# Where the tiles of a fused transformer kernel begin in SBUF: small ones first, large ones at multiples of 1024 bytes

## The reference

```
x = x + tanh(g_xattn[0]) * L0_xattn(ctx, ctx, layernorm(x))   # 16 heads of 16, softmax over the HEADS
x = x + tanh(g_ffn[0])   * L0_ffn(layernorm(x))               # silu(x Wg') * (x Wu') Wd', hidden 768, int weights / 127
x = x + tanh(g_xattn[1]) * L1_xattn(layernorm(x), ctx)        # 16 query heads, one key/value head, softmax over the context
x = x + tanh(g_ffn[1])   * L1_ffn(layernorm(x))               # x (W + lora)' + b
```

## Time and profile before

| | |
|---|---|
| time, median of 3 runs | 2446.94 us (2446.25 to 2447.63) |
| span of the profiled execution, first to last instruction | 2442.8 us, so 4.1 us less than the median |
| the 58 rounds of the loop, at 36.31 us each | 2106 us of the span |
| PE busy | 97% |
| DVE, POOL, ACT busy | 90%, 73%, 70% |
| granted TensorE clock | 0.996 of full speed, that is 2.4 GHz |

### The profile page before, as it was taken

The page is one execution under the profiler, slowest core; times in us unless marked ns, Lnnn a source line. Parts: engine busy times, 40 slices in busy tenths (PEclk is TensorE's granted clock), DMA queues, the critical chain, the costliest instruction groups (busy, mean ns, idle before and its releaser), DMA issues.

```text
span 2442.8 us, 70142 instructions
## 1 busy us (share of the span) xinstructions
PE 2357.7 (97%) x27814; PEld 2081.6 (85%) x27814; DVE 2205.6 (90%) x3678; ACT 1719.5 (70%) x3402; POOL 1773.4 (73%) x2512
## 2 busy tenths in 40 slices
PE   6899999999999999999999999999999999999897
PEld 5788888888888888888888888888888888888786
DVE  6879999999999999999999999999999999999963
ACT  4567777777777777777777777777777777777664
POOL 3667777777777777787777777777777777777653
PEclk9999999999999999999999999999999999999999
DMA  3000010010011010011001000001001001101000
GB/s 106 25 19 29 28 35 24 28 35 24 28 35 30 22 35 30 26 31 30 28 28 30 28 28 31 28 28 35 24 28 35 24 28 35 30 22 35 17 19 15
DMA packets 74326, 73.26 MB, mean 30 GB/s; under 512 B 6555, under 2 KB 73393, under 8 KB 74290
## 3 DMA queue, kind: packets, MB, share of 16 engines
q1 hardware_dynamic: 74290, 72.75, 9.5%
HBM read 54.90 MB, written 16.78 MB: 29 GB/s over the span
## 4 chain that ended last, share of the span: by engine, by line
PE 64%; DVE 19%; ACT 7%; POOL 7%; issue 2%; DMA 0%; POOLq 0%; SPq 0%; DVEq 0%; ACTq 0%
PE work L2136 13%; PE work L2137 11%; PE work L2138 11%; DVE m L1517 6%; PE scores L2229 6%; PE scores L2239 5%; PE work L2272 5%; PE work L2175 4%; DVE scores L1523 4%; ACT e L857 3%; POOL zt L417 3%; PE scores L2218 3%; ACT xn_D L814 3%; PE work L2153 2%; PE work L2159 2%
## 5 line engine op out<-in xcount | busy, mean ns | idle before, releaser
L857 ACT ACTIVATE e<-scores 120x1024 f32<-120x1024 f32 x512 | 513.4, 1029 | 88.3 <-PE scores L2239 56.6
L2136 PE MATMUL work<-xt_hi_B,w_hi 128*128 128x256 f32 x1536 | 456.5, 297 | 3.8 <-DVE y_lo_A L1497 1.6
L2137 PE MATMUL work<-xt_lo_B,w_hi 128*128 128x256 f32 x1536 | 430.2, 280 | 0.0
L2138 PE MATMUL work<-xt_hi_B,w_lo 128*128 128x256 f32 x1536 | 430.0, 280 | 0.0
L417 POOL TENSOR_TENSOR zt<-e 120x512 f32<-120x512 f32 x256 | 328.7, 1285 | 118.1 <-ACT e L857 112.1
L411 POOL TENSOR_TENSOR h_lo<-h_f,h_hi 128x256 fp32r<-128x256 f32 x384 | 279.5, 735 | 147.3 <-ACT h_hi L807 147.1
L1517 DVE TENSOR_REDUCE m<-scores 120x128 fp32r<-120x2048 f32 x128 | 291.0, 2273 | 66.2 <-PE scores L2229 66.0
L2136 PEld LDWEIGHTS work<-xt_hi_B,w_hi 128*128 128x128 f32 x1536 | 289.3, 188 | 60.6 <-DVE h_f L1511 24.9
L1523 DVE TENSOR_TENSOR scores<-scores,m 120x1024 f32<-120x1024 f32 x256 | 302.8, 1227 | 4.3
L1535 DVE TENSOR_TENSOR e<-e,work 120x2048 f32<-120x2048 f32 x128 | 291.4, 2277 | 0.2
L2137 PEld LDWEIGHTS work<-xt_lo_B,w_hi 128*128 128x128 f32 x1536 | 289.9, 189 | 0.0
(11 more groups left out here) (256 smaller groups left out, 7283.5 us busy)
## 6 DMA issues: line engine op xcount, KB each, us to landing
x_ln<-xp SPq DMA_DIRECT2D x64, 256.0 KB, 2.7
x_res<-xp SPq DMA_DIRECT2D x64, 256.0 KB, 2.7
y<-y_out SPq DMA_DIRECT2D x64, 256.0 KB, 2.2
ctx_f_A<-cp SPq DMA_DIRECT2D x64, 128.0 KB, 2.5
ctx_f_C<-cp SPq DMA_DIRECT2D x64, 128.0 KB, 2.0
qm<-mT SPq DMA_DIRECT2D x256, 4.0 KB
e<-wi SPq DMA_DIRECT2D x3, 768.0 KB, 5.5
w_ctx<-wc SPq DMA_DIRECT2D x1, 656.0 KB
```

The costliest lines, as they stand in the source:

```text
L857: return act.activation(e[0:SC, c, 2 * h:2 * h + 2, :, :].rearrange("p a b n -> p (a b n)"), scores[0:SC, 2 * h:2 * h + 2, :].rearrange("p ...
L2136: pe.matmul(out, a_hi, b_hi_, start=first, stop=False, skip_group_check=parts)
L2137: pe.matmul(out, a_hi, b_lo_, start=False, stop=False, skip_group_check=parts)
L2138: last = pe.matmul(out, a_lo, b_hi_, start=False, stop=end, skip_group_check=parts)
```

## The change

The code that runs is the same: each engine has the same instructions in the same order with the same waits and sizes. What differs is the order of the allocations, and with it the byte at which each tile begins. Six groups of small tiles (`stats`, `mv`, `var_eps`, `neg_mean`, `shift`, `rstd`, four each, for the layer norms) come first and take 896 bytes. The large tiles follow, each with a size that is a multiple of 1024 bytes except `ident` and `neg_ident` (512 each). The other small tiles, and `w_ctx` of 5248 bytes, come last. A tile `masks` that nothing used is gone.

| tile (bytes in a partition) | begins at, before | remainder by 1024 before | begins at, after | remainder after |
|---|---|---|---|---|
| w_hi (28672) | 16512 | 128 | 17408 | 0 |
| w_lo (28672) | 45184 | 128 | 46080 | 0 |
| neg_ident (512) | 74400 | 672 | 75264 | 512 |
| x_ln (2048); up to xt_lo_D all the same remainder | 88608 | 544 | 83968 | 0 |
| xt_hi_A (2048) | 117280 | 544 | 112640 | 0 |
| xt_hi_B (2048) | 119328 | 544 | 114688 | 0 |
| ctx_f_A (1024); up to v0_pad the same | 134592 | 448 | 129024 | 0 |
| e0, e1 (16384) | 152128, 168512 | 576 | 146432, 162816 | 0 |
| y_hi_A, y_hi_C, h_hi, h_lo | 202432, 204480, 216768, 222912 | 704 | 196608, 198656, 210944, 217088 | 0 |
| w_ctx (5248) | 77056 | 256 | 223232 | 0 |

With 704 as the beginning, a piece of 512 bytes begins at 704 or at 192; with 544, at 544 or at 32; in `w_hi`, at 128 or at 640. So in steps of 64 bytes the tiles from `x_ln` to `xt_lo_D` begin 32 bytes off a step, and `w`, `y` and `h` on a step. After the change every one of these pieces begins at 0 or 512.

```diff
--- before.py
+++ after.py
@@ -88,26 +88,22 @@
             return ctx.enter_context(nc.semaphore(name))
...
 
+        stats = {s: sb(f"stats_{s}", [P, NT, 6]) for s in "ABCD"}
+        mv = {s: sb(f"mv_{s}", [P, NT, 2]) for s in "ABCD"}
+        var_eps = {s: sb(f"var_eps_{s}", [P, NT]) for s in "ABCD"}
+        neg_mean = {s: sb(f"neg_mean_{s}", [P, NT]) for s in "ABCD"}
+        shift = {s: sb(f"shift_{s}", [P, NT]) for s in "ABCD"}
+        rstd = {s: sb(f"rstd_{s}", [P, NT]) for s in "ABCD"}
+
         w_hi = sb("w_hi", [P, WCOLS], F32R)
...
         ident = sb("ident", [P, P])
-        masks = sb("masks", [P, 2])
         neg_ident = sb("neg_ident", [P, P], F32R)
         wk0 = sb("wk0", [P, KC * D])
-        parity = sb("parity", [P, 2])
-        row_of = sb("row_of", [P, 4])
-        neg_row = sb("neg_row", [P, 2])
-        w_ctx = sb("w_ctx", [P, CCOLS])
         ones_k = sb("ones_k", [P, D], F32R)
-        bias_col = sb("bias_col", [P, 2 * KC])
-        key_bias = sb("key_bias", [P, 2, KC])
         bias_rows = sb("bias_rows", [P, 2, D])
...
         val_bias = sb("val_bias", [P, D])
-        minus_half = sb("minus_half", [P, NT])
-        eps_tile = sb("eps_tile", [P, NT])
-        zero_tile = sb("zero_tile", [P, NT])
-
         x_ln = sb("x_ln", [P, NT, D])
...
         x1 = sb("x1", [P, NT, D])
@@ -115,43 +111,27 @@
         x2_before = sb("x2_before", [P, NT, D])
...
         y_out = sb("y_out", [P, NT, D])
-
         xn = {s: sb(f"xn_{s}", [P, NT, D]) for s in "ABCD"}
...
         xt_lo = {s: sb(f"xt_lo_{s}", [P, KC, S], F32R) for s in "ABCD"}
-        stats = {s: sb(f"stats_{s}", [P, NT, 6]) for s in "ABCD"}
-        mv = {s: sb(f"mv_{s}", [P, NT, 2]) for s in "ABCD"}
-        var_eps = {s: sb(f"var_eps_{s}", [P, NT]) for s in "ABCD"}
-        ln_count = sb("ln_count", [P, 1])
-        neg_mean = {s: sb(f"neg_mean_{s}", [P, NT]) for s in "ABCD"}
-        shift = {s: sb(f"shift_{s}", [P, NT]) for s in "ABCD"}
-        rstd = {s: sb(f"rstd_{s}", [P, NT]) for s in "ABCD"}
-
         ctx_f = {s: sb(f"ctx_f_{s}", [P, KC, P]) for s in "AC"}
-
         qt = {st: sb(f"qt_{st}", [P, KC * S]) for st in "A"}
...
         qm1 = sb("qm1", [P, 2, KC * S])
-
         v0_pad = sb("v0_pad", [P, H // 2, 64])
-        v1_one = sb("v1_one", [P, 2 * HD])
         m0 = sb("m0", [P, 2, P], F32R)
...
         mT = sb("mT", [P, S])
-
         e0 = sb("e0", [P, NT, 4, 4, P])
-
         e1 = sb("e1", [P, KC, 4, 2, S])
...
         yz_q = sb("yz_q", [P, KC, 2, S // 32, 2 * HD])
-        rz_q = sb("rz_q", [P, KC, 2, S // 32])
         y_q = sb("y_q", [P, KC, S // 32, 2, HD])
         y1f = sb("y1f", [P, KC, S])
-        bias_row = y1f[0:1, :, :].rearrange("p k n -> p (k n)")
         y_hi = {s: sb(f"y_hi_{s}", [P, KC, S], F32R) for s in "AC"}
...
         th = sb("th", [P, 2, S])
@@ -159,6 +139,23 @@
         h_f = sb("h_f", [P, 2, S])
...
         h_lo = sb("h_lo", [P, HC, S], F32R)
+
+        w_ctx = sb("w_ctx", [P, CCOLS])
+        parity = sb("parity", [P, 2])
+        row_of = sb("row_of", [P, 4])
+        neg_row = sb("neg_row", [P, 2])
+        bias_col = sb("bias_col", [P, 2 * KC])
+        key_bias = sb("key_bias", [P, 2, KC])
+        minus_half = sb("minus_half", [P, NT])
+        eps_tile = sb("eps_tile", [P, NT])
+        zero_tile = sb("zero_tile", [P, NT])
+        ln_count = sb("ln_count", [P, 1])
+        v1_one = sb("v1_one", [P, 2 * HD])
+        rz_q = sb("rz_q", [P, KC, 2, S // 32])
+        tg = sb("tg", [P, 4])
+        graw = sb("graw", [P, 4])
+
+        bias_row = y1f[0:1, :, :].rearrange("p k n -> p (k n)")
 
...
         e1_flat = e1[:, :, :, :, :].rearrange("p a b c d -> p (a b c d)")
@@ -172,8 +169,6 @@
         t2_s = e1_flat[0:50, small + 3 * D:small + 4 * D]
...
         luT_s = e1_flat[0:4, small + 4 * D + 4:small + 4 * D + 54]
-        tg = sb("tg", [P, 4])
-        graw = sb("graw", [P, 4])
 
...
```

## The result

The changed kernel takes 2458.35 us (median of 5 runs, 2458.01 to 2459.22), the kernel before, measured beside it, 2446.25 us (median of 5, 2443.48 to 2447.63). The ratio is 1.0047, with a 95% interval of 1.0035 to 1.0059: 12 us slower, where 2432 us was forecast. The change made the kernel slower, and it did so in the way of the rival called Collision (2462 us): all the large products now run at the slow pace.

The account below looks back on a forecast made before the run. PE was taken to bound the kernel, with 64% of the chain. Saving 0.24 us in each of 58 rounds gives 14 us, plus 1 us outside the loop: 2446.9 to 2432 us, with an 8-in-10 range of 2418 to 2463.

Parts of the forecast that it names:

- Collision: Rival: weights and stream on the same remainder collide whatever their bytes; all products 0.120 us, 15 us slower, 2462; chance 0.23.
- The other engines at zero: POOL, DVE, ACT and DMAs costed at no change; 0.5% of their 33% of the chain would be 4 us either way.
- the reading of the hand-over: Epilogue, `rows_out` C to `keep_busy`: a distance of 0.11 us was taken to mean 0.1133 for all products after the change.
- A place that is 32 bytes off a step of 64 costs: In fp32r matmuls, such a place costs 4 ns as the stream and 7 ns as the weights.
- The lower bound of 0.107: Estimate for product distances: half of plain fp32's 0.213 us in `values0`, if the present remainder of 128 has a price.
- The sum by stretches: Savings counted over four parts of a loop round: 0.27 us, 0.24 after lead-ins, 14 us over 58 rounds.
- stretch 2: 1202.5 to 1212.5 us, `gate_up` 3 to 5 and attention, PE sets the pace; 0.144 us counted as saved.
- stretch 4: 1224.2 to 1232.6 us, `rows_out` A to `rows_out` D, PE sets the pace; 0.128 us counted as saved.
- stretch 1: 1196.3 to 1202.5 us, `gate_up` 0 to 2, PE waits for the exponential; its 0.14 us saving counted as lost.
- Stretch 3: 1212.5 to 1224.2 us, `down`, `rows_out` C, `queries` C, under PE's 0.46 us wait for xn_D; 0 counted.
- The slack at `gate_up` 5: At 1208.70 us its weight load stands behind `h_f`; 0.12 us of slack, enough for the 0.096 saved in `gate_up` 3 and 4.
- The wash: Rival: aligned products settle at a second pace, 0.117, taken over from what ran before, or nothing changes; 2447 to 2448; chance 0.27.

Follow-up runs that it names:

- The map: Changed kernel with 28 rows of 33 extra fp32r matmuls ahead of the loop, weights and stream at varied places; 2571.0 us, added rows included.
- the second map: Changed kernel with other added matmul rows: differences around 64, alternating pairs of places, 512-column streams, plain fp32; 2544.6 us in one run.
- the last version: Changed kernel with 64 bytes behind w_lo and xt of A, B, C allocated last, so every product has relation 64; 2436.64 us, 0.9960 of the kernel before.

## Why the prediction was wrong

By its own steps:

- "Only places of tiles change", and the profile shows a time that depends on a tile's place: right. `rows_out` A at 0.113 beside `rows_out` D at 0.120 was the effect, read ahead of the run, and the products in the stretches where PE sets the pace give 0.14 of the 0.16 us that a round lost.
- The other engines at zero: right. DVE is busy 2205.7 us against 2205.6, and on POOL `y_lo_C` takes 1273 ns against 1274 while `xt_lo_B` went from 1268 to 1275, about the 0.5% that the prediction allowed for.
- **The step that failed** is the reading of the hand-over: "One row tells them apart ... that distance is 0.11". The two observations were the right ones, and they gave two theories, same remainder and same bytes. I let one distance between two different relations decide, `rows_out` C to `keep_busy`. The map shows that such a distance is of a run that hasn't settled, and that weights 8192 bytes away collide as much as the same bytes. In the trace of before, the starts in nanoseconds show it at the same place: 114 at the hand-over and 119 and 120 behind it. In the second map, pairs whose own relation is 64, but whose next weights lie 0 or 128 from the running stream, settle at 118.8: a relation that one hand-over doesn't show costs time in a settled run. What the runs show in the place of the 0.1133 for all products is 0.120 wherever a run with the same remainders has settled, and a round of 36.467 us where 36.07 was forecast. Without this step, what was left was `keep_busy` with 8 distances of 0.120, the only run whose remainders were those of all products to come. The rival built on it, at 0.23, should have been the likeliest case.
- "A place that is 32 bytes off a step of 64 costs": wrong as a cause. 32 bytes off is the relation 96 or 160, and 0 is as bad as 160. The name I gave to the effect (off a step) hid that a place has no price by itself.
- The lower bound of 0.107 from plain fp32 found nothing: no run settled below 0.113.
- The sum by stretches: right in its form. The rival's account was 0.10 in stretch 2, 0.11 in stretch 4, 0.05 in stretch 1, together 0.26 a round; measured about 0.04, 0.09 and 0.01, together 0.14 of the round's 0.16. It is too high where the runs start unsettled, so that the price isn't paid by each of 12 matmuls, and in stretch 1, which is cushioned nearly whole. Stretch 3 cost nothing, as said: its loss shortened the wait for xn_D from 0.46 to 0.27. 58 x 0.16 = 9.3 us, and 12.1 between the medians.
- The slack at `gate_up` 5 was not tried by the result, since PE became slower; its weight load waits 0.41 for `h_f` in both kernels.
- The wash was right in one thing: that a run has a second pace. `rows_out` C kept 117.8 at relation 64 in each version that had it. That it takes this pace over from what ran before is not borne out: the last version has runs that go from 118 to 113 and back at the same relation. And aligned products settle at 120, not there.
- The Trainium skill's rule, weighed in the rival ("SBUF — State Buffer", section "A bandwidth-pool intuition that's wrong (but worth ruling out)"), is that weight loads have a second independent read port. The map is against what I drew from it: the same matmul takes 113.3 or 120.0 ns by nothing but where its weights begin in relation to its stream. Nor do the lines of 16 bytes that the same page of the Trainium skill gives (in "Specifications (TRN2)", and not in "Terms", which the prediction names as well) sort the values: 0, 64, 96 and 160 are all multiples of 16, and take 120, 113, 117 and 120.

What stays open: why the relation matters, with this pattern by 256 bytes; what chooses between 113 and 118 at relations 64 and 192; and the 3 us outside the rounds, of which the clock accounts for some in the profiled executions.

## What to carry to other kernels

For fp32r matmuls of 128x128 weights and 256 columns, a tile's place was neither good nor bad by itself: what counted was where the weights begin minus where the stream begins, and making everything begin at a multiple of 256 bytes was among the worst choices (120 ns, against 113 or 118 at a difference of 64). Where PE sets the pace, try a pad of 32 to 128 bytes between the tiles that meet in a matmul, and time it; here that was 0.6%, for no instruction. When two theories are left, read them off runs that have settled, and not off the one distance at a change; and if the only settled run that is like the kernel to come speaks for the loss, forecast the loss.

## What the hardware showed that was not expected

- The distance of an fp32r matmul with 256 columns follows the difference of two addresses, and over the 512 bytes tried it repeats by 256: 120.0 ns at 0, 256 and 512; 113.3 at 64 and 113.4 at 320; 120.0 at 112, 120.1 at 160; and about 117 to 119 at the other differences tried. At 60 and 68 the 113 is gone (119 and 118).
- It has two paces. At relation 64 a run settles at 113.3 or at 117.8 and stays there for 33 matmuls; at 192 too (113 and 118 in two rounds of one execution). `rows_out` D at 192 ran at 113.5 behind a run at 113, and `rows_out` A at the same 192 ran at 117.8; but with all relations at 64 `queries` C settled at 113 behind a run at 118, and `down` at 118 behind that. What chooses is open.
- A run behind other work mostly needs 4 to 10 matmuls until it is settled (from 2 to 11 in the rows of the maps), so a run of 12 shows only a part of the effect.
- Plain fp32 (215 to 216 ns for 256 columns) shows nothing of it.
